# A two-layer graph attention network with a routed FFN: 20 of 49 tiles take their FFN inside the second edge phase

## The reference, cut to what matters

```python
def gat(x, src, dst, W, a_src, a_dst, b, heads, concat):          # N = 6250 nodes, 200000 edges + self loops
    h = (x @ W).reshape(n, heads, -1)                             # D = 256
    e = leaky_relu((h*a_src).sum(-1)[src] + (h*a_dst).sum(-1)[dst], 0.2)
    ex = exp(e - segment_max(e, dst)[dst])
    alpha = ex / (segment_sum(ex, dst)[dst] + 1e-16)
    return segment_sum(h[src] * alpha[:, :, None], dst) + b       # concat (layer 1) or mean (layer 2)

x = x + gat(elu(gat(layernorm(x), ..., 4 heads)), ..., 1 head)
y = layernorm(x)
p = softmax(y @ gate_w + gate_b)                                  # 8 experts, the top 2 of each node count
out = x + sum over e of p_top2[:, e] * (gelu(y @ W1[e] + b1[e]) @ W2[e] + b2[e])   # 256 -> 512 -> 256
```

## Time and profile before

| | before |
|---|---|
| time, median of 3 runs | 4746.47 us (4742.43 to 4746.71) |
| profiled execution, first to last instruction | 4740.9 us |
| busy over that span | PE 3346.1 us (71%), PEld 2411.6 (51%), DVE 2922.4 (62%), ACT 1673.7 (35%), POOL 3342.4 (71%) |
| mean granted clock of PE | 0.757 of full |
| end of edge phase 2, first instruction of the routing | 4196.6 us |
| first load of the combine phase, end | 4683.27 us, 4740.9 us |

### The profile page before, as it was taken

One profiled execution on the slowest core, in us unless ns is written; L12 is line 12 of the kernel. 1 busy time (PEld: TensorE's weight loads), 2 busy tenths in 40 slices (PEclk: granted clock), 3 DMA queues, 4 the chain that ended last, 5 costly groups with the idle time before them and its releaser, 6 DMA issues. The chain is left out here.

```text
span 4740.9 us, 66856 instructions
## 1 busy us (share of the span) xinstructions
PE 3346.1 (71%) x12675; PEld 2411.6 (51%) x12676; DVE 2922.4 (62%) x7641; ACT 1673.7 (35%) x3999; POOL 3342.4 (71%) x3623
## 2 busy tenths in 40 slices
PE   6577676666676666674667777677777667759994
PEld 5455454444554444453455555455555455537673
DVE  7766666666666666666666666666666666654445
ACT  4333333333333333332333333333333333322223
POOL 5777777777777777776777777777777777747323
PEclk8777777777777777777777676767777777769997
DMA  5555555555555555544555555555555555554325
GB/s 162 141 139 140 139 140 138 140 139 140 140 140 140 138 139 140 139 127 123 144 146 146 145 144 145 146 146 145 145 144 144 145 145 145 147 171 143 94 82 192
DMA packets 312156, 669.34 MB, mean 141 GB/s; under 512 B 74233, under 2 KB 137653, under 8 KB 311812
## 3 DMA queue, kind: packets, MB, share of 16 engines
q0 software_dynamic: 170464, 468.31, 37.1%
q1 hardware_dynamic: 141039, 199.89, 14.6%
q10 hardware_dynamic: 596, 0.53, 0.0%
HBM read 601.32 MB, written 75.12 MB: 143 GB/s over the span
## 5 line engine op out<-in xcount | busy, mean ns | idle before, releaser
L1155 POOL DMA_INDIRECT rows<-table,idx x3192 | 3017.8, 945 | 981.2 <-issue 925.8
L1311 PE MATMUL bank<-rows,hit 128*128 128x260 f32 (+1 forms) x6448 | 2494.9, 544 | 1191.1 <-DVE acc L1426 1180.0
L1311 PEld LDWEIGHTS bank<-rows,hit 128*128 128x128 f32 x6448 | 1645.9, 272 | 1740.2 <-DVE acc L1426 1370.0
L1411 DVE TENSOR_TENSOR rows<-rows,bank 128x1024 f32<-128x1024 f32 x808 | 947.7, 1214 | 36.9 <-ACT rows L1191 36.9
L1188 ACT ACTIVATE arg<-arg 128x32 f32<-128x32 f32 (+1 forms) x404 | 88.4, 219 | 2383.3 <-DVE arg L1404 2383.3
L1426 DVE TENSOR_TENSOR acc<-acc,bank 128x260 f32 (+1 forms) x2016 | 842.4, 418 | 30.6 <-PE bank L1311 3.0
L1397 DVE TENSOR_TENSOR arg<-rows,bank 128x32 f32<-128x32 f32 (+1 forms) x404 | 71.6, 177 | 1155.1 <-DMA rows<-table,idx 1154.8
L1377 DVE TENSOR_TENSOR hit<-bank,dst_at 128x256 f32<-128x256 f32 x1616 | 672.0, 417 | 0.0
L1182 ACT ACTIVATE hit_t<-gap,ones 128x1024 bf16<-128x1024 bf16 x404 | 463.8, 1148 | 27.3
L1175 ACT ACTIVATE gap<-loc,minus_node 128x1024 bf16<-128x1024 bf16 x404 | 462.7, 1145 | 10.9 <-DMA loc<-loc_row 10.6
L1296 PEld LDWEIGHTS bank<-du,hit_t 128*128 128x128 bf16 x3232 | 249.2, 109 | 248.7 <-issue 180.1
(11 more groups left out here) (289 smaller groups left out, 2249.2 us busy)
## 6 DMA issues: line engine op xcount, KB each, us to landing
loc<-loc_row SPq DMA_DIRECT2D x404, 256.0 KB, 3.6
rows<-table,idx POOLq DMA_INDIRECT x3192
sent<-zeros SPq DMA_DIRECT2D x202, 68.3 KB
xe<-sent SPq DMA_DIRECT2D x106, 128.5 KB
got<-back SPq DMA_DIRECT2D x48, 256.0 KB, 5.2
fw<-in_L_ffn_W SPq DMA_DIRECT2D x16, 512.0 KB
table<-acc POOLq DMA_DIRECT2D x49, 130.0 KB
table<-acc SPq DMA_DIRECT2D x49, 128.5 KB, 2.3
```

The costliest lines, as they stand in the source:

```text
L1155: pool.indirect_dma_start(rows[:, way, n, 0:R], None, table, bass.IndirectOffsetOnAxis(idx[:, way, n:n + 1], 0)).then_inc(rows_in[way], 16)
L1311: last = nc.tensor.matmul(sum_bank[(way + m) % 4][:, 0:R], hit[:, way, n, :], rows[:, way, n, 0:R], start=(n == UNITS[m][0]), stop=(n == U ...
L1411: nc.vector.tensor_tensor(r, r, weight[:, some, :].unsqueeze(3).to_broadcast([P, PIECE, H, D // H]), ALU.mult).then_inc(scaled, 1)
```

## The change

1. The 20 tiles that are finished first (DENSE) go in five groups of four (GROUP) through all eight experts inside edge phase 2, from step 34 (DENSE_AT) for 5 x 32 = 160 steps. Four steps take one expert for one group: with `way` 2 and 3 the four chunks of the up product (`dense` part 0 and 1: two f32 matmuls of 512 columns each), with `way` 0 and 1 the four tiles of the down product (part 2 and 3: a bias matmul and four matmuls of 256 columns each). All go through one PSUM bank. ACT applies Gelu to a chunk (`bend`), DVE weighs a tile with the gate's share and adds it to `total` (`take_down`).
2. `spread_du` moves on PE from between the halves to ahead of unit 1; of each step's two dense pieces one stands behind it and the other, for the next step, ahead of unit 4.
3. ACT loads the Gelu table and, after `bend`, the Exp table (through `exp_table_first`). `weigh` in layer 2 writes one Exp, and DVE copies the weights to PSUM (`weight_staged`).
4. SP loads the weights of one expert at a time (512 KB up, 512 KB down, single buffers) and loads and stores `total`.
5. LAG is 4 in both layers; the partial tile is ranked last; two tiles instead of one are finished behind the last step.
6. The routing, expert and combine phases see the other 29 tiles (TAIL): T falls from 106 to 66, the scatters from 98 to 58, the combine tiles from 49 to 29. ACT first copies the 29 tiles' rows to a buffer in order of rank (`move_y`), and POOL's output stores look their tile up.

The core of the diff:

```diff
-    LAG = 3
+    LAG = 4
+    DENSE_AT = 4 * 8 + 2
+    PER_GROUP = EXPERTS * SETS
...
+        def grouped(eng, body, first, groups, ahead=False):
...
+            for s in range(first):
+                body(s, s % SETS, s // SETS, *dense_of(s))
+            with eng.Fori(0, groups) as g:
+                for n in range(PER_GROUP):
+                    s = first + n
+                    body(g * PER_GROUP + s, s % SETS, g * EXPERTS + s // SETS, *dense_of(s, g))
...
+                def load_up(e, n):
+                    if not number(n) or n >= 1:
+                        sp.wait_ge(up_made, n * CHUNKS)
+                    sp.dma_start(up_w[:, :, :], fw1[e].rearrange("(c p) n -> p c n", p=P)).then_inc(up_w_in, 16)
...
                     act.wait_ge(bounded, s + 1)
-                    nc.scalar.activation(weight, a, ACT.Exp, scale=-1.0)
+                    if first_layer:
+                        nc.scalar.activation(weight, a, ACT.Exp, scale=-1.0)
                     nc.scalar.activation(rows[:, way, :, D:D + H], a, ACT.Exp, scale=-1.0).then_inc(weight_ready, 1)
...
+                def bend(at, c):
...
+                    act.wait_ge(up_made, n * CHUNKS + c + 1)
+                    nc.scalar.activation(inner[:, c, :], dense_bank[:, :], ACT.Gelu,
+                                         bias=up_b[:, e * CHUNKS + c:e * CHUNKS + c + 1]).then_inc(inner_ready, 1)
...
                         make_hit_t(s + 2, (way + 2) % SETS, turn * 2 + (way + 2) // 2)
+                    if bends:
+                        bend(at, 2 * at[2])
+                        bend(at, 2 * at[2] + 1)
+                        nc.scalar.activation(exp_first[:, :], kp.ones[:, 0:1], ACT.Exp)
                     if not number(s) or s + 1 < STEPS:
                         weigh(s + 1, (way + 1) % SETS)
...
+                def dense(at, half):
+                    g, e, part, n = at
+                    if part < 2:
+                        c = 2 * part + half
+                        if c == 0:
+                            pe.wait_ge(up_w_in, n * 16 + 16)
+                            pe.wait_ge(down_taken, n * GROUP + 1)
...
+                        else:
+                            pe.wait_ge(inner_ready, n * CHUNKS + c)
+                        for kc in range(2):
+                            last = nc.tensor.matmul(
+                                dense_bank[:, :], up_w[:, kc, c * P:(c + 1) * P],
+                                turned_y[:, kc, bass.ds(g * GROUP, GROUP), :].rearrange("p a n -> p (a n)"),
+                                start=(kc == 0), stop=(kc == 1))
+                        last.then_inc(up_made, 1)
+                    else:
+                        i = 2 * (part - 2) + half
...
+                            pe.wait_ge(down_taken, n * GROUP + i + 1)
+                        nc.tensor.matmul(dense_bank[:, 0:D], kp.ones[0:1, :], down_b[:, :], start=True, stop=False)
+                        for c in range(CHUNKS):
+                            last = nc.tensor.matmul(dense_bank[:, 0:D], inner[:, c, i * P:(i + 1) * P], down_w[:, c, :],
+                                                    start=False, stop=(c == CHUNKS - 1))
+                        last.then_inc(down_made, 1)
...
+                    def spread_ahead():
+                        if not number(s) or s + 2 < STEPS:
+                            spread_du(s + 2, (way + 2) % SETS)
+                        if at is not None:
+                            dense(at, 1)
+                    def dense_ahead():
+                        if next_at is not None:
+                            dense(next_at, 0)
...
+                        sum_rows(s, way, 0, {1: spread_ahead})
+                        sum_rows(s, way, 1, {4: dense_ahead})
...
+                    if piece == 0 and not first_layer:
+                        nc.vector.tensor_copy(weight, rows[:, way, :, D:D + H]).then_inc(weight_staged, 1)
+                        dve.wait_ge(weight_staged, to_next)
...
+                def take_down(at, half):
...
+                    dve.wait_ge(down_made, n * GROUP + i + 1)
+                    nc.vector.scalar_tensor_tensor(total[:, i, :], dense_bank[:, 0:D], share_of[:, i, e:e + 1],
+                                                   total[:, i, :], ALU.mult, ALU.add).then_inc(down_taken, 1)
...
+                    if at is not None:
+                        take_down(at, 0)
                     if ahead:
                         keep_du(s + 1, nxt, to_here)
+                    if at is not None and at[1] == 0 and at[2] == 0:
+                        gate_tops(at)
+                    if at is not None and at[1] == 0 and at[2] == 1:
+                        gate_shares(at)
+                    if at is not None:
+                        take_down(at, 1)
...
+                    at = act.value_load(kp.order[0:1, DENSE + t:DENSE + t + 1], min_val=0, max_val=NT - 1)
+                    nc.scalar.copy(fb.rows[:, t, 0:D], kp.acc[:, at, 0:D]).then_inc(y_moved, 1)
```

More of the change, by code:

```diff
@@ new lines, in dense @@
+                def dense(s, at):
+                    if number(s) and s == 12:
+                        with nc.allow_non_contiguous_dma(reason="biases along the partitions"):
+                            sp.dma_start(up_b[:, :], fb1.rearrange("e (c p) -> p (e c)", p=P)).then_inc(up_b_in, 16)
+                    if number(s) and s == 24:
+                        load_up(0, 0)
+                    if number(s) and s == 26:
+                        load_down(0, 0)
+                    if number(s) and s == DENSE_AT + 1:
+                        sp.wait_ge(mid_out, 16 * GROUP)
+                        for h in range(2):
+                            load_total(0, h)
+                    if at is None:
+                        return
+                    g, e, part, n = at
+                    if part == 0 and not (number(n) and n == 0):
+                        load_up(e, n)
+                    if part == 2 and not (number(n) and n == 0):
+                        load_down(e, n)
@@ L1250, in ride, with step @@
                         keep_y(turn - LAG)
-                def step(s, way, turn):
+                def step(s, way, turn, at=None):
+                    bends = at is not None and at[2] < 2
                     if not number(s) or s + 3 < STEPS:
@@ L1300, in spread_du, with sum_rows @@
                         last.then_inc(spread, 1)
-                def sum_rows(s, way, half):
+                def sum_rows(s, way, half, before=None):
                     pe.wait_ge(scaled, s * PIECES + half + 1)
                     for m in units_of(s, half):
+                        if before is not None and m in before:
+                            before[m]()
                         if m == 4:
@@ L1696, in load @@
                         sp.wait_ge(home_ready, k - 1)
-                    if not number(k) or turn * 4 + after < NT:
+                    if not number(k) or turn * 4 + after < TAIL:
                         sp.wait_ge(second_sent[after % 4], (turn + after // 4 + 1) * 16)
```

375 lines of the change are left out of this document (283 added, 92 removed).

## The result

The changed kernel takes 4822.0 us (median of 4 runs, 4818.0 to 4828.7), the kernel before 4745.8 us (median of 4 runs, 4742.4 to 4746.7): 1.0166 of it, with a 95% interval from 1.0153 to 1.0178. The forecast was 4690 us and faster. The profiled execution has a span of 4816.3 us and a mean granted clock of 0.852 (0.757 before).

A forecast was written before the change was run, and what follows sets the result against it. POOL's gathers were taken to bound the edge phase at 10.0 us a step, PE the expert phase. From 4746.5, -164 - 15 + 10 + 112 gave 4689.5 us, with a range of 4590 to 4840.

The forecast's parts named there:

- -164 us for 40 work items: Expert phase: 40 work items fewer on PE at 4.10 us each, -164 us.
- -15 us for the combine phase: Combine phase: 20 tiles fewer to store on POOL, less the new look-up for 29 tiles; 23 to 6 us gained, 15 taken.
- +10 us at the ends: Ends of both layers: with LAG 4 one more tile finished after the last step, +10 us, between 5 and 15.
- Start of the routing unchanged: Routing start: ACT's copies by rank run under the expert weight load at no cost; without that cover up to 18 us.
- SP's blocked loads and 1 MB a turn at nothing: Dense steps: loads of `loc` behind SP's new waits and 24 GB/s more traffic cost nothing; a late step 10 us a turn.
- Full clock in the 160 steps: Dense steps: PE, working some 8.9 us of a step, runs at full clock; the rival at 0.71 gave 4850 us, chance 0.12.
- A rule against it (the drain): Dense steps: a drain after each ACT table load would add 102 us, time 4792; chance 0.03.
- 160 steps at 43.0 us a turn, +112 us: Dense steps: four steps take 43.0 us against POOL's 40.0, 120 us in 40 turns, the first 8 us not seen.
- 8 for the four buffers: Edge phase 2: POOL's four row buffers hide the first 8 us of the dense steps' added time.
- allowance for waits, 0.35 us a turn: Dense steps: some two added waits a step, 0.05 us each, raise the turn from 42.65 to 43.0 us.
- waits and look-ups take 0.5 us of a step: Dense steps: loop registers and SP's blocked loads cost 0.5 us a step, not 0.1; 64 us more, 4754; chance 0.18.
- break-even step of 11.1 us: Dense steps: a chain 0.36 us longer than forecast uses up the 57 us of gain over 160 steps.

The follow-up runs named there:

- e8: Changed kernel with only the first expert's dense weights loaded whole, the other weight loads of the 160 steps cut to 32 columns each: 4823.9 us.
- e3: Changed kernel with Relu in place of Gelu in the dense work of edge phase 2: 4769.8 us.
- e2: Changed kernel with DVE taking a step's second down product behind the attention argument instead of ahead of it: 4698.3 us.
- e6: Changed kernel with loops written out, second take behind the argument, and ACT computing attention weights between a step's two Gelus: 4579.3 us.

## Why the prediction was wrong, step by step

- **-164 us for 40 work items**: right, -163.2, at 4.10 us an item. **-15 us for the combine phase**: the size is right, -14.7, in part by luck: a store costs POOL (15.8 + 26.8) / 29 = 1.47 us now, 0.29 more than before, which is the middle of the two bounds (nothing and 0.6) between which the forecast chose without a row. **+10 us at the ends**: +11.8.
- **Start of the routing unchanged, SP's blocked loads and 1 MB a turn at nothing**: right. From the first instruction of the routing to the first expert product it is 42.4 us, 41.9 before; e8 takes most of the bytes out without a gain, and the waits show none for SP's queue.
- **Full clock in the 160 steps**: the level was right (0.96, forecast 0.9 or more), but its price of nothing was not: the missing 4% fall in the main on the down product that the chain waits for, and the steps that they touch are 44 us longer.
- **A rule against it (the drain)**: rightly given 0.03; e3 prices a load at 1.3 us.
- **160 steps at 43.0 us a turn, +112 us**: this is the step that failed. The mechanism was right: two chains, one through `take_down`, one through the weights, and e2, e3 and e6 show each of them. Its size was not: 46.3 us, and +241.5 instead of +112. Between steps 34 and 194 it is 254 us where 120 were forecast; outside of it 12.6 us come back, where the forecast had 8 for the four buffers. Three terms were missing or small. (1) The pieces of the turn, by 60 us. The forecast put the spread 0.2 us behind `keep_du`, as if PE stood ready; in ways 3 and 0 unit 4, the finished tile's product and unit 0 are still ahead of it in PE's order, 0.95 and 0.7 us. The rest are a few tenths for the down piece, the take and the way from DVE to PE, and the forecast's allowance for waits, 0.35 us a turn, is already taken off. 27 of the 60 us go when the loops are written out. (2) The passes of the loop, 28 us, which the forecast had at nothing. (3) The clock, 44 us, also at nothing.
- **The rival "waits and look-ups take 0.5 us of a step"** named registers of the 32-step loop and was the nearest, at 4754 us; the measured excess over the forecast is 134 / 160 = 0.84 us a step. The break-even step of 11.1 us was right to work with: the steps take 11.56, and the time is 76 us above before.
- The range up to 4840 us held the time, but the likeliest value was 132 us too low and the direction was the wrong one.

Two things stay open: what in PE's work lets the clock fall in one step and not in the next of the same form, and how much of the 4.75 us stall is the fetching of instructions. The profile calls it "issue", the experiments tie it to the loops, and a fetch is seen inside it.

## What to carry to other kernels

When work is put into the slack of a phase, sum the loop of each engine in its own program order, with the waits between, and not only the chain that looks longest. Here a product that DVE had to take before its argument tied two engines that could have run side by side, and moving one instruction was worth 124 us. Place the taker where its engine would wait anyway, and put latency-critical small work (the weights) ahead of bulk work (the second Gelu) on a shared engine. A stall costs in full only on an engine whose chain sets the pace, so shorten the chains first; what the loops cost shrank from 65 us to about 6 without their being touched.

## What the runs showed of the hardware

- A new pass of a loop with 32 steps in it made its first step 8.4 us longer: 2.64 us of idle time without a releaser on DVE, then 4.75 on PE in the middle of its first matmuls of the pass, with a 16 KB packet on an instruction queue inside, then matmuls at half clock. Written out, it cost nothing.
- The same eight matmul records of 256 columns take 1.99 us or 3.5 us within a few steps of each other. Steps that were partly at half clock were 1.3 to 1.5 us longer in ways 0 and 1, and in the profile with the idle time behind the product filled there were 43 of them instead of 34.
- A matmul with one row as weights and 256 columns took 0.31 us a record, where one of 128 rows takes about 0.22 to 0.25 in the same pieces.
- A table load that an experiment takes away can stay for another function's sake: Relu in place of Gelu removed one Exp load of two, since Sqrt had taken its place.
